# Linear attention and expert-routed gated attention on one core: VectorE splits the low-rank part ahead of the expert state additions, and TensorE computes the next tile's denominators behind the intra-chunk products

## The chip, the cores and the metric

The kernel runs on one core of a Trainium2 chip. The metric is device time in microseconds (us) from launch to end. A core has five engines that run their own instruction streams and meet only at semaphores: TensorE (PE in the rows, PEld for its weight loads), VectorE (DVE), ScalarE (ACT), GpSimd (POOL) and SyncE (SP, which here only issues loads and stores). Within one engine the instructions start in the order in which they are written, so an instruction that waits holds back all that stand behind it.

## The reference, cut to what matters

The input is x of shape 2 x 4096 x 512. Two residual blocks follow each other; `ln` is a layer norm without weights.

```python
x = x + ln(attention(ln(x)))     # linear attention, 16 heads of 32
x = x + ln(ffn(ln(x)))           # gated linear attention with 4 experts

# attention: q, k rectified
z   = 1 / (sum_n(k) . q + eps)                 # the "denominators"
out = (context @ q) * z @ w_proj.T + b_proj

# ffn
q1, k1, v = x @ Wq, x @ Wk, x @ Wv
q2 = x @ Wqa @ Wqb                              # low-rank
k2 = softmax(x @ Wka @ Wkb)
gk1, gk2 = log_sigmoid(x @ Wg1a @ Wg1b + bg1) / 16, log_sigmoid(x @ Wg2a @ Wg2b + bg2) / 16
e = softmax(x @ We); mask = one_hot(top_1(e))   # the router
o = gla(q1, k1, v, gk1) + sum over experts of gla(q2*e*mask, k2*e*mask, v, gk2*mask)
g = x @ Wga @ Wgb
return (rmsnorm(o) * silu(g)) @ Wo
```

`gla` is a recurrence over time, `S_t = diag(exp(gk_t)) S_(t-1) + k_t^T v_t`, `o_t = q_t S_t`. The dense path has one state, and the expert path has four.

## The kernel before, in words

For each of the two batch elements the kernel makes two passes over 32 tiles of 128 rows. The first pass builds keys, moments and queries of the linear attention. The second pass takes one tile after the other and carries the state of the recurrence from tile to tile; it is the pass that the change touches. Its loop body `step(n, p, front, back, ahead)` is written once for each engine and works on three tiles at a time:

- **ahead**, tile n+1: the linear attention's output and the first residual. TensorE computes the denominators (`den`, line 312, into PSUM bank 3), ScalarE turns them into reciprocals (`ahead_z`, lines 647 and 649, as exp(-ln)), VectorE multiplies the queries by them (`ahead_qz`, line 1211), TensorE projects (`y_mm`).
- **front**, tile n: the projections of the second block. TensorE computes the low-rank part (`low_rank`), ScalarE takes it out of PSUM (lines 654 to 656), VectorE splits it into a high and a low fp16 half (`front_low`, lines 1115 to 1122) and routes (`front_router`, lines 1126 to 1145). TensorE's gates (`gates`, line 350) wait for `low_ok`, which VectorE sets at line 1122. `label_bc` (line 346) spreads the router's label over the partitions, VectorE makes masks from it (`front_masks`, line 1151 on), and `project_k` on TensorE waits for these, since it overwrites the label's bank.
- **back**, tile n-1: what the recurrence adds. TensorE multiplies by the states (`inter`, line 448) and by the masked scores (`intra`, line 457), ScalarE squares the result (`back_square`, line 719), VectorE sums, normalises, gates and splits it (lines 1222, 1226, 1230, 1063, 1065), and TensorE transposes it (`og_transpose`, line 466) and projects it (`out_mm`). At the head of a step VectorE masks the scores (`back_masks`, line 1082, `back_masks2`, line 1090) and adds the state products of the dense path (`back_carry1`, line 1099) and of the experts (`back_carry`, line 1106, two instructions of 64 x 1024). GpSimd masks the queries (`back_qm`, line 959) and adds the two score tensors (`back_am`, line 965).

The order of the work is written out by hand: each engine runs its pieces in the order of the calls in its own `step`. On ScalarE that order is `front_ke`, `ahead_z(n + 1)`, `back_square(m)`, `front_sig_high`, `back_rms`. On VectorE it is, behind the router and the masks: `front_kmax`, `front_kdiff`, `front_logsig`, `ahead_qz`, `back_norm`, `front_lslow`, `back_normed`, `back_gated`, `back_split`. The first tile of each batch element runs without back, the last without ahead; 60 of the 64 steps have all three parts, 62 have front and back.

Two semaphore values are set so that a first wait passes: `cur(n)` is n+2 and `prev(n)` is n+1. In `step`, m is n-1 and mp is 1-p.

Of the kernel before, what the change touches and what calls it, by code (L numbers as in the profile page):

```python
# [64 lines left out]
def sandwich_kernel(nc, x_d, wqkv_d, wproj_d, bproj_d, wb_d, wl_d, ws_d, wo_d, nw_d, consts_d, out_d):  # L65
# [11 lines left out]
    with ExitStack() as ctx:  # L77
# [146 lines left out]
        def cur(n):  # L224
            return n + 2
# [69 lines left out]
        def _(pe):  # L295
# [179 lines left out]
            def step(n, p, front=True, back=True, ahead=True):  # L475

                m, mp = n - 1, 1 - p
                if front:
                    low_rank(n)
                    project_v(n)  # L480
                    gates(n)
                    project_k2(n)
                if ahead:
                    den(n + 1, mp)
                if front:
                    label_bc(n)
                if back:
                    inter(m)
                    intra(m, mp)
                if front:  # L490
                    project_k(n)
                    project_q(n)
                if back:
                    og_transpose(m)
                if front:
                    cumulate(n)
                if back:
                    out_mm(m)
                if front:
                    half_sums(n)  # L500
                if ahead:
                    y_mm(n + 1)
                if front:
                    transposes(n)
                    state_products(n, p, ahead)
                    scores(n, 0)
                if ahead:
                    xn_transpose(n + 1)
                if front:
                    scores(n, 1)  # L510
# [521 lines left out]
        def _(dve):  # L1032
# [91 lines left out]
            def front_router(n):  # L1124
                dve.wait_ge(S("low0_ok"), cur(n))
                ve.reduce_max(lmax[:, :], logit_s, X).then_inc(S("lmax_ok"), 1)
                dve.wait_ge(S("lmax_ok"), n + 1)
                ve.tensor_scalar(ldiff[:, :], logit_s, lmax[:, :], None, ALU.subtract).then_inc(S("ldiff_ok"), 1)
                dve.wait_ge(S("ldiff_ok"), n + 1)

                ve.scalar_tensor_tensor(lscore[:, :], ldiff[:, :], 0.0, score, ALU.is_equal, ALU.mult).then_inc(S("lscore_ok"), 1)
                dve.wait_ge(S("lscore_ok"), n + 1)
                ve.reduce_max(lab[:, :], lscore[:, :], X).then_inc(S("lab_ok"), 1)
                dve.wait_ge(S("lab_ok"), n + 1)
                dve.wait_ge(S("rx_pe"), prev(n))
                ve.tensor_scalar(lab_i[:, :], ident, lab[:, :], None, ALU.mult).then_inc(S("labi_ok"), 1)
                dve.wait_ge(S("vm_ok"), prev(n))
                ve.tensor_scalar(m4[:, :], score, lab[:, :], None, ALU.is_equal).then_inc(S("m4_ok"), 1)
                dve.wait_ge(S("m4_ok"), n + 1)
                dve.wait_ge(S("sum_pe"), prev(n))  # L1140
                ve.tensor_tensor(hm[:, :, :], wide(m4[:, :], 2), halves.unsqueeze(1).to_broadcast([P, NEXP, 2]), ALU.mult).then_inc(S("hm_ok"), 1)  # L1141
                dve.wait_ge(S("lexp_ok"), cur(n))
                ve.reciprocal(rr[:, :], lsum[:, :]).then_inc(S("rr_ok"), 1)
                dve.wait_ge(S("rr_ok"), n + 1)
                ve.tensor_scalar(rq[:, :], rr[:, :], D2 ** -0.5, None, ALU.mult).then_inc(S("rq_ok"), 1)
# [97 lines left out]
            def step(n, p, front=True, back=True, ahead=True):  # L1243
                m, mp = n - 1, 1 - p
                if back:
                    back_masks(m)
                    back_carry1(m)
                    back_masks2(m)
                    back_carry(m)
                if front:  # L1250
                    front_low(n)
                    front_router(n)
                    front_masks(n)
                    front_kmax(n)
                    front_kdiff(n)
                    front_logsig(n)
                if ahead:
                    ahead_qz(n + 1, mp)
                if back:
                    back_norm(m)  # L1260
                if front:
                    front_lslow(n)
                if back:
                    back_normed(m, mp)
                    back_gated(m, mp)
                    back_split(m)
                if front:
                    front_kfac(n)
                    front_sil(n, p)
                if ahead:  # L1270
                    ahead_qz_split(n + 1)
                if front:
                    front_gated_1(n)
                    front_gated_q2(n)
                if back:
                    back_out(m, mp)
                if front:
                    front_decay(n, p)
                if ahead:
                    ahead_residual(n + 1, mp)  # L1280
                    ahead_low(n + 1, mp)
# [147 lines left out]
```

## Time and profile before

| | |
|---|---|
| median of 3 runs | 3148.73 us |
| the runs | 3140.97, 3148.92, 3148.73 us |
| the profiled execution | 3142.66 us |
| its span, first to last instruction | 3140.8 us |
| its mean granted TensorE clock | 0.944 of full speed |
| TensorE busy | 2876.9 us (92% of the span) |
| VectorE, ScalarE, GpSimd busy | 1962.6, 1639.7, 1355.5 us |

Some 1.9 us of the profiled execution lie outside its span. Busy times of TensorE are of modelled ends and count work at half clock as busy, so the share of 92% doesn't say that it runs at its peak. The idle time of an engine is listed with what ended it. Where a row names a line, it is the line of the kernel before; after the change the lines of TensorE stand one lower from `inter` on, and those of VectorE one lower up to the router's `hm` and one higher behind it.

### The profile page before, as it was taken

Reading aid. Unit: us, or ns where it says so; the run is one execution under the profiler, and the core shown is the slowest. Engines: PE = TensorE matmul, PEld = TensorE weight load, DVE = VectorE, ACT = ScalarE, POOL = GpSimd, SP = SyncE. Lnnn points to the kernel's source line nnn. Section 1 sums busy time; section 2 is a strip of 40 time slices with the busy share of each in tenths; the row PEclk is TensorE's granted clock in tenths of the full one; section 3 lists DMA queues with packets and bytes.
Section 4 is the critical chain, followed back from the end, with each engine's and each line's share of the span. In section 5 each row is a group of like instructions: output and inputs, shape, how many; then the busy total and the mean of one; then the engine's idle time right before and its main releaser. Section 6 shows DMA issues by size and latency. Waiting matters only on the chain.

```text
span 3140.8 us, 56322 instructions
## 1 busy us (share of the span) xinstructions
PE 2876.9 (92%) x20720; PEld 1830.1 (58%) x20720; DVE 1962.6 (62%) x3878; ACT 1639.7 (52%) x3281; POOL 1355.5 (43%) x1006
## 2 busy tenths in 40 slices
PE   6999899999999999999879988999999999999997
PEld 3444566666666666666534445666666666666665
DVE  4442666667666676666544426666667666666675
ACT  4332555555555565555433325555556555555553
POOL 2873444444444444444322334444444444444443
PEclk9999999999999999999889999999999999999999
DMA  4121000000000000000021110000000000000000
GB/s 171 61 94 41 18 20 20 20 20 20 20 20 20 20 20 20 20 20 20 18 85 57 67 41 18 20 20 20 20 20 20 20 20 20 20 20 20 20 20 11
DMA packets 48376, 97.49 MB, mean 31 GB/s; under 512 B 5376, under 2 KB 5376, under 8 KB 47680
## 3 DMA queue, kind: packets, MB, share of 16 engines
q1 hardware_dynamic: 37008, 68.44, 6.5%
q10 hardware_dynamic: 9792, 17.83, 1.5%
q0 software_dynamic: 1520, 10.50, 0.8%
q8 instruction: 32, 0.52, 0.1%
q14 instruction: 24, 0.20, 0.0%
HBM read 63.19 MB, written 33.55 MB: 31 GB/s over the span
## 4 chain that ended last, share of the span: by engine, by line
PE 77%; DVE 16%; ACT 3%; issue 3%; POOL 1%; DVEq 0%; DMA 0%; POOLq 0%; SPq 0%; ACTq 0%
PE psum L303 12%; PE psum L448 11%; PE psum L304 11%; PE psum L305 11%; PE psum L547 5%; DVE region L1106 5%; PE psum L437 4%; PE psum L312 4%; PE psum L457 4%; PE psum L413 3%; DVE region L1090 3%; PE psum L353 2%; PE psum L423 2%; ACT ogT L730 2%; PE psum L352 2%
## 5 line engine op out<-in xcount | busy, mean ns | idle before, releaser
L977 POOL TENSOR_TENSOR region<-region,kfac 128x512 f32<-128x512 f32 x64 | 66.8, 1043 | 842.3 <-DVE kfac L1190 842.3
L448 PE MATMUL psum<-region 128*128 128x128 f32 x2560 | 352.2, 305 | 10.8 <-POOL region L959 10.8
L448 PEld LDWEIGHTS psum<-region 128*128 128x128 f32 x2560 | 346.1, 221 | 14.5 <-issue 11.1
L959 POOL TENSOR_TENSOR region<-region,mb 128x512 f32<-128x512 f32 x256 | 322.7, 1292 | 73.3 <-ACT region L620 72.9
L992 POOL TENSOR_TENSOR region<-region,decay 64x1280 f32<-64x1280 f32 x128 | 298.3, 2330 | 117.9 <-DVE decay L1206 112.9
L972 POOL TENSOR_SCALAR region<-region,m 128x512 f32<-128x512 f32 x256 | 172.9, 697 | 285.7 <-DVE hm L1141 210.5
L303 PE MATMUL psum<-wb,region 128*128 128x512 f16 x768 | 292.4, 381 | 3.3 <-DVE mb L1155 3.3
L304 PE MATMUL psum<-wb,region 128*128 128x512 f16 x768 | 292.0, 380 | 0.0
L305 PE MATMUL psum<-wb,region 128*128 128x512 f16 x768 | 291.7, 380 | 0.0
L951 POOL TENSOR_TENSOR region<-region 128x1024 f32<-128x1024 f32 x64 | 146.7, 2292 | 287.4 <-DVE region L1302 229.9
L1302 DVE SCALAR_TENSOR_TENSOR region<-psum,region 128x512 f16<-128x512 f32 x64 | 44.3, 692 | 261.0 <-ACT region L791 261.0
L730 ACT ACTIVATE ogT<-psum 128x1024 f16<-128x1024 f16 x64 | 65.5, 1024 | 241.5 <-PE psum L466 241.5
L671 ACT ACTIVATE region<-psum 128x1536 f32<-128x1536 f32 x64 | 92.9, 1452 | 184.7 <-PE psum L353 184.7
L547 PE MATMUL psum<-region 128*128 128x512 f16 x768 | 176.2, 379 | 0.0
L350 PE MATMUL psum<-ws,region 128*128 128x512 f16 x128 | 40.4, 398 | 141.0 <-DVE region L1122 141.0
L1106 DVE TENSOR_TENSOR region<-psum,region 64x1024 f32<-64x1024 f32 x128 | 155.7, 1217 | 0.9
L1072 DVE SCALAR_TENSOR_TENSOR region<-psum,rstd,region 128x512 f32<-128x512 f32 x64 | 48.0, 751 | 170.0 <-ACT rstd L616 170.0
L965 POOL TENSOR_TENSOR region<-region 128x1024 f32<-128x1024 f32 x64 | 150.4, 2350 | 0.0
L423 PE MATMUL psum<-region 64*128 64x128 f32 x2048 | 148.2, 284 | 0.0
L423 PEld LDWEIGHTS psum<-region 64*128 64x128 f32 x2048 | 124.1, 187 | 31.1 <-issue 24.6
L612 ACT ACTIVATE og<-psum 128x512 f32<-128x512 f32 x128 | 76.4, 597 | 123.5 <-PE psum L305 123.5
L620 ACT ACTIVATE region<-psum 128x512 f32<-128x512 f32 x256 | 137.6, 589 | 0.0
(233 smaller groups left out, 7580.7 us busy)
## 6 DMA issues: line engine op xcount, KB each, us to landing
region<-x_in SPq DMA_DIRECT2D x128, 256.0 KB, 2.7
q_cols<-region ACTq DMA_DIRECT2D x64, 256.0 KB, 2.4
region<-q_cols SPq DMA_DIRECT2D x64, 256.0 KB, 2.9
out_rows<-region SPq DMA_DIRECT2D x60, 256.0 KB, 2.0
region<-wb_in POOLq DMA_DIRECT2D x1, 3072.0 KB, 11.2
region<-wqkv_in SPq DMA_DIRECT2D x4, 512.0 KB, 6.2
region<-wqkv_in POOLq DMA_DIRECT2D x2, 1024.0 KB, 5.6
region<-wproj_in POOLq DMA_DIRECT2D x2, 1024.0 KB, 7.4
```

The lines of the kernel that those rows point to most:

```text
L303: mm(out, lhs(0), rhs(0), start=start, stop=False)
L304: mm(out, lhs(0), rhs(1), start=False, stop=False)
L305: return mm(out, lhs(1), rhs(0), start=False, stop=stop)
L423: last = mm(bank[where[odd]][:, pr * P:(pr + 1) * P], kT[h, pr, :], qT[h, pr, :], start=True, stop=True)
L448: last = mm(bank[7][:, pr * P:(pr + 1) * P], q, state[:, pr, path, :], start=(pr == 0 and path == 0), stop=False, skip_group_check=True)
L547: last = mm(bank[4 + j], xn8[:, p * GT + t, x * C + j * P:x * C + (j + 1) * P], k16[:, y_, :], start=first and begins, stop=final and ends ...
L951: nc.gpsimd.tensor_tensor(kacc, kacc, k16, ALU.add).then_inc(S("kacc_ok"), 1)
L959: last = nc.gpsimd.tensor_tensor(qm[:, e, :, :], q2T, mb[:, e, :].unsqueeze(1).to_broadcast([P, PAIRS, P]), ALU.mult)
L965: nc.gpsimd.tensor_tensor(am1[:, :, :, :], am1[:, :, :, :], am2[:, :, :, :], ALU.add).then_inc(S("am_ok"), 1)
L972: last = nc.gpsimd.tensor_scalar(vm[:, e, :], v[:, p, :], m4[:, e:e + 1], 1.0, ALU.mult, ALU.mult)
L992: nc.gpsimd.tensor_tensor(state[h, :, :, h], carry[h, :, :, :], decay[h, :, :].unsqueeze(3).to_broadcast([D2, PAIRS, PATHS, D2]), ALU.mult ...
L1106: last = ve.tensor_tensor(carry[h, :, 1:PATHS, :], psum[h, 2:4, :].rearrange("p a (r e d) -> p (a r) e d", r=2, e=NEXP), state[h, :, 1:PAT ...
```

## The change

It reorders three things in the second pass and changes no instruction. On TensorE, `den(n + 1, mp)` moves from ahead of `label_bc(n)` to behind `intra(m, mp)`. On VectorE, `back_carry(m)` moves from ahead of `front_low(n)` to behind `front_router(n)`. The last two instructions of the router (the reciprocal of the softmax sum and its scaled copy) become `front_prob(n)` and move from ahead of `front_masks(n)` to behind `front_kdiff(n)`. The streams of ScalarE, GpSimd and SyncE are as before.

```diff
--- before.py
+++ after.py
@@ -480,13 +480,12 @@
                     project_v(n)
                     gates(n)
                     project_k2(n)
-                if ahead:
-                    den(n + 1, mp)
-                if front:
                     label_bc(n)
                 if back:
                     inter(m)
                     intra(m, mp)
+                if ahead:
+                    den(n + 1, mp)
                 if front:
                     project_k(n)
                     project_q(n)
@@ -1139,6 +1138,8 @@
                 dve.wait_ge(S("m4_ok"), n + 1)
                 dve.wait_ge(S("sum_pe"), prev(n))
                 ve.tensor_tensor(hm[:, :, :], wide(m4[:, :], 2), halves.unsqueeze(1).to_broadcast([P, NEXP, 2]), ALU.mult).then_inc(S("hm_ok"), 1)
+
+            def front_prob(n):
                 dve.wait_ge(S("lexp_ok"), cur(n))
                 ve.reciprocal(rr[:, :], lsum[:, :]).then_inc(S("rr_ok"), 1)
                 dve.wait_ge(S("rr_ok"), n + 1)
@@ -1246,13 +1247,16 @@
                     back_masks(m)
                     back_carry1(m)
                     back_masks2(m)
-                    back_carry(m)
                 if front:
                     front_low(n)
                     front_router(n)
+                if back:
+                    back_carry(m)
+                if front:
                     front_masks(n)
                     front_kmax(n)
                     front_kdiff(n)
+                    front_prob(n)
                     front_logsig(n)
                 if ahead:
                     ahead_qz(n + 1, mp)
```

TensorE in the loop's body, before, from the last product of `project_k2` on (`kden` are the denominators' weights, `lab_i` the label, `wb` the big projection's weights; a row with no wait named follows from the one above it):

```order
L352 MATMUL psum<-ws,region 128x512 [waits v_ok]
L353 MATMUL psum<-ws,region 128x512
L308 ISA
L312 MATMUL psum<-region,kden 128x128 [waits carry_ok,qb0_in]
L312 MATMUL psum<-region,kden 128x128 x3
L346 MATMUL psum<-lab_i,ones 128x128 [waits am1_ok,labi_ok]
L448 MATMUL psum<-region 128x128 [waits qm_ok,state_ok,out_ok]
L448 MATMUL psum<-region 128x128 x19
L457 MATMUL psum<-region 128x64 [waits am_ok]
L457 MATMUL psum<-region 128x64 x7
L303 MATMUL psum<-wb,region 128x512 [waits mb_ok]
```

The same place after the change:

```order
L352 MATMUL psum<-ws,region 128x512 [waits v_ok]
L353 MATMUL psum<-ws,region 128x512
L346 MATMUL psum<-lab_i,ones 128x128 [waits am1_ok,labi_ok]
L448 MATMUL psum<-region 128x128 [waits qm_ok,state_ok,out_ok]
L448 MATMUL psum<-region 128x128 x19
L457 MATMUL psum<-region 128x64 [waits am_ok]
L457 MATMUL psum<-region 128x64 x7
L308 ISA
L312 MATMUL psum<-region,kden 128x128 [waits carry_ok,qb0_in]
L312 MATMUL psum<-region,kden 128x128 x3
L303 MATMUL psum<-wb,region 128x512 [waits mb_ok]
```

The denominators (L312) stood ahead of the label, the states and the scores; they now stand behind all three and directly ahead of `project_k`, with the wait for `carry_ok` that they carry.

VectorE at the head of the loop's body, before, from the second half of the second score mask on (`low1_ok` is ScalarE's eviction of the low-rank part):

```order
L1090 TENSOR_TENSOR region<-psum,same_c 128x512
L1106 TENSOR_TENSOR region<-psum,region 64x4x256 x2
L1111 REGISTER_ALU
L1115 CAST region<-region 64x2x128 [waits q1_pe,low1_ok]
L1116 CAST region<-region 64x2x128
L1117 CAST region<-region 32x128
```

The same place after the change:

```order
L1089 TENSOR_TENSOR region<-psum,same_c 128x512
L1110 REGISTER_ALU
L1114 CAST region<-region 64x2x128 [waits q1_pe,low1_ok]
L1115 CAST region<-region 64x2x128
L1116 CAST region<-region 32x128
L1119 TENSOR_TENSOR region<-region 32x128 [waits lowh_ok]
```

The expert state additions (L1106) are gone from between the score masks and the first cast, which waits for ScalarE.

VectorE further on, before, from the router's label columns `m` to the log-sigmoid that `project_q` and `front_sig_high` wait for:

```order
L1138 TENSOR_SCALAR m<-cst,lab 128x4 [waits vm_ok]
L1141 TENSOR_TENSOR hm<-m,cst 128x8 [waits sum_pe,m4_ok]
L1143 RECIPROCAL rr<-lsum 128x1 [waits lexp_ok]
L1145 TENSOR_SCALAR rq<-rr 128x1 [waits rr_ok]
L1151 SCALAR_TENSOR_TENSOR same_d<-psum,lab,cst 128x128 [waits cum_pe,rx_pe]
L1152 SCALAR_TENSOR_TENSOR same_c<-psum,lab,cst 128x128
L1155 TENSOR_SCALAR mb<-psum 128x128 [waits qm_ok]
L1155 TENSOR_SCALAR mb<-psum 128x128 x3
L1176 TENSOR_REDUCE kmax<-psum 128x8 [waits k2_pe]
L1182 TENSOR_TENSOR region<-psum,kmax 128x512 [waits k2g_ok,kr_ok,kmax_ok]
L1162 SCALAR_TENSOR_TENSOR region<-psum,region 128x1536 [waits sil_ok,sum_pe,ln_ok]
```

The same place after the change:

```order
L1140 TENSOR_TENSOR hm<-m,cst 128x8 [waits sum_pe,m4_ok]
L1105 TENSOR_TENSOR region<-psum,region 64x4x256 x2
L1152 SCALAR_TENSOR_TENSOR same_d<-psum,lab,cst 128x128 [waits cum_pe,rx_pe]
L1153 SCALAR_TENSOR_TENSOR same_c<-psum,lab,cst 128x128
L1156 TENSOR_SCALAR mb<-psum 128x128 [waits qm_ok]
L1156 TENSOR_SCALAR mb<-psum 128x128 x3
L1177 TENSOR_REDUCE kmax<-psum 128x8 [waits k2_pe]
L1183 TENSOR_TENSOR region<-psum,kmax 128x512 [waits k2g_ok,kr_ok,kmax_ok]
L1144 RECIPROCAL rr<-lsum 128x1 [waits lexp_ok]
L1146 TENSOR_SCALAR rq<-rr 128x1 [waits rr_ok]
L1163 SCALAR_TENSOR_TENSOR region<-psum,region 128x1536 [waits sil_ok,sum_pe,ln_ok]
```

The state additions (now L1105) stand behind `hm`, the router's last step, and ahead of the masks, and the reciprocal that waits for ScalarE's `lexp_ok` stands ahead of the log-sigmoid instead of ahead of the masks.

## Rows read from the trace of the kernel before

**Rows 1.** What line 350 of TensorE waited for: us in all, number of times.
```profile
  DVE region L1122: 141.0, 62
```
**Rows 2.** TensorE in one tile: start, duration, operation [idle before, released by].
```profile
823.92 0.60 PE L350 MATMUL psum<-ws,region 128*128 128x512 f16 x2 [2.28 <-DVE region L1122]
...
825.69 2.07 PE L312 MATMUL psum<-region,kden 128*128 128x128 f32 x8
...
832.78 1.90 PE L457 MATMUL psum<-region 128*128 128x64 f32 x16
...
834.52 0.38 PE L303 MATMUL psum<-wb,region 128*128 128x512 f16 x1
...
840.34 0.61 PE L466 MATMUL psum<-ident,og 128*128 128x128 f16 x8
```
**Rows 3.** VectorE in the same tile, same columns.
```profile
817.70 1.29 DVE L1090 TENSOR_TENSOR region<-psum,same_c 128x512 f32<-128x512 f32 x2
...
818.90 2.45 DVE L1106 TENSOR_TENSOR region<-psum,region 64x1024 f32<-64x1024 f32 x2
...
821.38 0.90 DVE L1115 CAST region<-region 64x256 f16<-64x256 f32 x1
...
823.57 0.29 DVE L1122 TENSOR_TENSOR region<-region 64x128 f16<-64x128 f32 x1
...
825.20 0.17 DVE L1141 TENSOR_TENSOR hm<-m,cst 128x8 f16<-128x8 f32 x1
...
829.93 0.69 DVE L1182 TENSOR_TENSOR region<-psum,kmax 128x512 f32<-128x512 f32 x1
...
830.54 1.75 DVE L1162 SCALAR_TENSOR_TENSOR region<-psum,region 128x1536 f32<-128x1536 f32 x1
```
**Rows 4.** ScalarE in the same tile: the end of the low-rank eviction.
```profile
819.41 0.27 ACT L655 ACTIVATE region<-psum 128x128 f32<-128x128 f32 x1
```
**Rows 5.** GpSimd in the same tile: the sum of the masked scores.
```profile
819.78 2.35 POOL L965 TENSOR_TENSOR region<-region 128x1024 f32<-128x1024 f32 x1
```
**Rows 6.** All 64 instances of line 1115: shortest, median, longest ns, first start.
```profile
L1115 DVE CAST region<-region x64: 285/893/906, 325.5 to 3083.1; 64x256 f16<-64x256 f32 x64
```
**Rows 7.** First pass: all instances of line 1298, same columns.
```profile
L1298 DVE TENSOR_TENSOR region<-region x64: 691/1767/1775, 15.2 to 1817.8; 128x512 f16<-128x512 f32 x64
```
**Rows 8.** First pass, one tile: GpSimd's line 951 and VectorE's line 1298.
```profile
1701.78 2.36 POOL L951 TENSOR_TENSOR region<-region 128x1024 f32<-128x1024 f32 x1 [5.99 <-DVE region L1302]
...
1702.92 1.76 DVE L1298 TENSOR_TENSOR region<-region 128x512 f16<-128x512 f32 x1 [0.77 <-ACT region L804]
```
**Rows 9.** ScalarE in the tile of rows 2: reciprocal denominators and the square.
```profile
831.20 0.64 ACT L647 ACTIVATE psum<-psum,eps_z 128x512 f32<-128x512 f32 x1
...
831.87 0.58 ACT L649 ACTIVATE psum<-psum 128x512 f32<-128x512 f32 x1
...
834.72 0.60 ACT L719 ACTIVATE og<-psum 128x512 f32<-128x512 f32 x1 [2.26 <-PE psum L457]
```
**Rows 10.** VectorE in the same tile: from the denominators to the split output.
```profile
832.49 1.12 DVE L1211 SCALAR_TENSOR_TENSOR region<-region,ksum_q,psum 128x128 f32<-128x128 f32 x4 [0.20 <-ACT psum L649]
...
835.35 0.69 DVE L1222 TENSOR_REDUCE oms<-og 128x8 f32<-128x512 f32 x1 [1.74 <-ACT og L719]
...
837.44 0.68 DVE L1226 TENSOR_TENSOR og<-psum,ors 128x512 f32<-128x512 f32 x1
...
839.34 0.69 DVE L1065 TENSOR_TENSOR og<-og 128x512 f16<-128x512 f32 x1
```
**Rows 11.** Stretches cut where TensorE starts line 350 again: length, TensorE busy, granted clock, DMA share, GB/s.
```profile
358.79:395.47 36.68, 34.13 (x279) 1.00 0.07 23
823.92:862.19 38.27, 35.71 (x278) 0.96 0.06 21
784.12:823.92 39.80, 37.24 (x279) 0.91 0.06 20
358.79:1520.23 1161.44, 1084.88 (x8340) 0.94 0.06 21
```

## The prediction

> **What bounds the kernel now.** I read the page first: TensorE is busy for 92% of the span and leads the chain of waits. I then took the list of what each TensorE line waited for. In the second pass one entry stands out: line 350, the first gate product, waits for line 1122, the last step of VectorE's low-rank split, 62 times for 141.0 us, or 2.27 us a time [rows 1]. The timeline of one tile on the four engines shows how it comes about. TensorE is through with its projection at 821.64 (823.92 less 2.28) and stands until 823.92 [rows 2]. VectorE masks the scores until 818.99, adds the expert states from 818.90 for 2.45 us, and starts the first cast of the split at 821.38; the split ends at 823.86 [rows 3]. The cast's own input is ready earlier: ScalarE ends the eviction at 819.68 [rows 4].
>
> The last view is the granted clock, in stretches cut where line 350 starts again. A tile without any stretch at the lower level (1.2 GHz) takes 36.68 us; others take 38.27 us at a mean of 0.96 and 39.80 us at 0.91 [rows 11]. The clock falls around the time at which TensorE starts again behind the 2.28 us. The mean over the 30 intervals of a batch element is 1161.44 / 30 = 38.71 us, so the halved clock costs 2.0 us a tile over and above the idle time.
>
> So the idle time ahead of the gates costs up to 2.3 us directly and 2.0 us by the clock. Everything behind it hangs on TensorE until the transpose of line 466 at 840.34 [rows 2]. There a second chain arrives nearly at the same time: VectorE's split of the output ends at 839.34 + 0.69 = 840.03 [rows 10]. It has 0.3 us to spare.
>
> **Part 1: VectorE's state additions behind the router.** Their 2.45 us leave the place ahead of the cast. The cast can't start before 819.68, so at best the split starts at 819.7 instead of 821.38.
>
> That supposes that the cast takes its own time only, and this is where I expect the gain to be lost. Of the 64 instances of line 1115 the shortest, the first tile's at 325.5, takes 285 ns, and the median takes 893 ns [rows 6]. In the shown tile it runs from 821.38 to 822.28, and GpSimd's addition of the two score tensors runs from 819.78 to 822.13 [rows 5]; in the first tile there is no such addition. The cast's end is GpSimd's end plus 0.15, which is its own 0.29 less 0.14. The first pass has the same pattern: line 1298 takes 691 ns alone and 1767 ns in the median [rows 7], and in one tile it ends at 1704.68, where GpSimd's line 951 ends at 1704.14 [rows 8]; 1704.14 + 0.69 - 0.14 is 1704.69. I read this as: a VectorE cast, or an addition with both inputs in SBUF, waits until a GpSimd instruction in flight is done.
>
> All six instructions of the split are of these kinds. After the change they are ready at 819.7, where GpSimd starts its 2.35 us. If GpSimd is first, the cast waits until about 821.99 and ends at 822.28, as before. If the cast slips in just ahead (0.29 us), GpSimd, ready since 819.0, takes its turn behind it, and the second cast waits instead, which ends within 0.1 us of where it ended before. Either way `low_ok` comes at 823.86 and the gates start at 823.92. Gain: 0 to 0.1 us; I take 0. If nothing waits, the split takes 2.48 (823.86 - 821.38) less the 0.61 that the cast loses now, and ends at 819.7 + 1.87 = 821.6. The gates then start when TensorE is ready, 2.2 us earlier. That is the other bound: 0 to 2.2 us a tile, besides the clock.
>
> The Trainium skill (SBUF — State Buffer, on the shared port pair) states that VectorE in a two-port mode, or with two SBUF inputs against a GpSimd instruction that reads SBUF, and GpSimd hold a shared port pair exclusively for a whole instruction, and that whoever is second fully blocks. The rows agree with it, to 0.01 us in the first pass. By this rule part 1 gains nothing; by the plain durations it would gain 2.2 us a tile and the clock.
>
> What moves with the additions: they now run from 825.4 (line 1141 ends at 825.37 [rows 3]) to 827.8. They read PSUM and one SBUF tensor, and ran beside GpSimd's addition at 1.22 us each before, so GpSimd's next work does not slow them. Behind them the masks start at about 827.85 instead of 827.9, since VectorE stood there for ScalarE's `lexp_ok` and for the label. The reciprocal pair adds some 0.35 us ahead of the log-sigmoid, where a wait of its own has long been over: that starts at about 830.8 instead of 830.54 [rows 3] and ends at 832.5. Who waits for it is `project_q` at 837 and `front_sig_high`, which is held longer by part 2. Cost: 0.
>
> **Part 2: the denominators behind the scores.** On TensorE nothing is added: the label, the states and the scores start about 1.86 us earlier, the denominators stand last, and `project_k` starts at 834.52 as before [rows 2]. Their end moves from 827.76 to about 834.52 + 0.2 = 834.7, 0.2 being the overlap that the old end had with the next product. The wait for `carry_ok` (827.8) is over by then.
>
> On ScalarE `ahead_z` waits for them, and `back_square` is queued behind it. Before, both halves of `ahead_z` were through by 832.45, and the square started at 834.72, 0.04 us behind the scores [rows 9]. Now it needs, from the denominators' end D: 0.04 for the semaphore, 0.67 to the second activation (831.87 - 831.20), 0.58 for that [rows 9]; the square then follows. VectorE's `ahead_qz` starts at D + 1.33 and holds VectorE for 1.12 us [rows 10], to D + 2.45, behind the square's end (D + 1.9). From there the chain is as before: line 1222 for 0.69, line 1171 for 1.15, and from the start of line 1226 to the end of line 1065 it is 840.03 - 837.44 = 2.59 [rows 10]. The sum is D + 6.88, or some 6.75 with the overlaps of 0.1 between neighbours that do not wait for one another. So `og_ok` comes at 841.45 to 841.6, and TensorE, which is ready for the transpose at 840.34, waits: 1.1 to 1.3 us a tile; I take 1.2. Queued behind that transpose is all the rest of TensorE's tile, and ScalarE and VectorE of that part follow it, so the whole tile is later by this much. The later work has room: the product `y_mm` starts 4.8 us behind the transpose and its input comes 3.3 us behind `og_ok`.
>
> **The sum.** Steps with all three parts: 60. Part 1: 0. Part 2: 60 x 1.2 = +72 us. The first tile of each batch element wins about 1 us, because its label no longer stands behind the denominators: -2. Made against the profiled execution, 3142.66 + 70 = 3213 us. That execution is 6 us below the median of 3148.73; the runs shown spread over 8 us. I forecast 3212.
>
> **What stays open** is the clock. The gap ahead of the gates stays, and so do the halved stretches; but which tile gets none, a short or a long one depends on where its gap falls, and the tile gets 1.2 us longer. If all tiles were of the 36.68 kind the period would be 37.9, which is -0.8 x 60 = -50 us against before; if all were of the 39.80 kind, 41.0 and +137 us. Neither end is likely, and half of each is: the forecast's own range is 3160 to 3265.
>
> **Rivals.**
> - The split is free of GpSimd (faster). The gates start 2.2 us earlier, the gap closes, and the clock stays up. Part 2 still costs its 1.2, since it hangs on the denominators and not on the gates. The tile takes 36.68 - 2.2 + 1.2 = 35.7, that is 3.0 less than 38.71: 3142.66 - 60 x 3.0 = 2963 us. For it: VectorE's six short instructions could keep their turn against a GpSimd instruction not yet begun. Against: rows 6 to 8, and that in the first pass each side gets in between two instructions of the other.
> - The longer wait ahead of the transpose halves the clock once more (slower still). It would join with the 0.25 us behind it. Price: 1.6 us (38.27 - 36.68) a tile for 60 tiles, +95 on the forecast: 3308. It decides when this gap acts like the one of 2.28. Against: no halving follows the 0.25 us.
> - Nothing moves: some 0.3 us of slack and a somewhat shorter gap cancel the new wait, 3143. For it speaks only that VectorE has idle time in each tile.
>
> **How the numbers follow.** Forecast with its own range: 0.74. Free split, or a part of it that spares the clock: 0.15. Clock halved again: 0.05. Nothing moves: 0.06. Less than about 0.3% (9 us) can't be told from no change here. A lucky mix of tiles gives 0.02 of the forecast's share to the faster side. So faster 0.17, same 0.07, slower 0.76. The range leaves out the free split and the second halving and reaches below the forecast's own range towards no change: 3135 to 3265.
>
> **What would show it.** Right: line 1114 still ends with GpSimd's addition, lasting about 2.5 us; line 350 still waits 2.3 us a tile for VectorE; ScalarE's first activation of `ahead_z` waits for TensorE's denominators; and line 465 waits 1.1 to 1.3 us for VectorE's line 1064. Wrong: line 1114 at 0.29 us with its first start at 819.7, a wait ahead of line 350 below 1 us, a granted clock near 1.0, or no wait ahead of line 465.

## The result, and the profile after

The changed kernel takes 3092.02 us in the median of 4 runs (3091.44 to 3092.17), the kernel before 3147.64 us over its 4 (3140.97 to 3148.92). The ratio is 0.9827, with a 95% interval of 0.981 to 0.9844: 55 us or 1.7% faster. The forecast was 3212 us, slower by 2%. It lies on the wrong side, and the measured time lies below the range.

The mean granted clock of the profiled execution, in its line with the span, is the first thing that differs; before it was 0.944:

```profile
core 0: 3090.3 us, clock 0.979
```

What the two lines of TensorE waited for (released by, us in all, times), from the lists of line 350 and of line 466 of the changed kernel. The first answers to [rows 1]:

```profile
  DVE region L1121: 126.1, 62
...
  DVE og L1064: 66.1, 62
```

The same list of line 466 in the kernel before:

```profile
  DVE og L1065: 9.2, 2
```

So the wait ahead of the gates shrank from 2.27 to 2.03 us a tile, no more. The two waits of line 466 that stood before, in the last tile of each batch element, are still there, and a new wait of (66.1 - 9.2) / 60 = 0.95 us stands ahead of the output's transpose in each of the other tiles. The transpose itself starts 1.08 us later: 15.91 us behind line 350 in a tile with the clock up, against 14.83 before. That is the forecast's own picture. TensorE in one tile (start, duration, operation [idle before, released by]), to be read against [rows 2]:

```profile
809.49 0.60 PE L350 MATMUL psum<-ws,region 128*128 128x512 f16 x2 [2.05 <-DVE region L1121]
...
811.26 4.68 PE L448 MATMUL psum<-region 128*128 128x128 f32 x40
...
815.78 1.90 PE L457 MATMUL psum<-region 128*128 128x64 f32 x16
...
817.52 1.11 PE L312 MATMUL psum<-region,kden 128*128 128x128 f32 x8
...
825.39 0.62 PE L466 MATMUL psum<-ident,og 128*128 128x128 f16 x8 [0.95 <-DVE og L1064]
```

The denominators now stand last of the four and take 1.11 us where they took 2.07; in this tile the clock is up. VectorE at the head of the next tile, against [rows 3, 6]:

```profile
841.03 1.29 DVE L1089 TENSOR_TENSOR region<-psum,same_c 128x512 f32<-128x512 f32 x2
...
842.97 0.32 DVE L1114 CAST region<-region 64x256 f16<-64x256 f32 x1 [0.65 <-ACT region L654]
...
843.30 2.35 DVE L1115 CAST region<-region 64x256 f16<-64x256 f32 x1
...
846.64 0.29 DVE L1121 TENSOR_TENSOR region<-region 64x128 f16<-64x128 f32 x1
...
848.26 0.17 DVE L1140 TENSOR_TENSOR hm<-m,cst 128x8 f16<-128x8 f32 x1
...
848.35 2.45 DVE L1105 TENSOR_TENSOR region<-psum,region 64x1024 f32<-64x1024 f32 x2
```

GpSimd's multiplications (line 958) and its addition of the score tensors there, against [rows 5]:

```profile
838.11 5.04 POOL L958 TENSOR_TENSOR region<-region,mb 128x512 f32<-128x512 f32 x4 [1.17 <-ACT region L619]
843.10 2.39 POOL L964 TENSOR_TENSOR region<-region 128x1024 f32<-128x1024 f32 x1
```

The first cast slips in ahead of it, in 0.32 us, and the second lasts 2.35 us, until 845.65: GpSimd's end, 845.49, plus 0.16. The split ends at 846.93, 0.25 us earlier in relation to GpSimd's addition than before (3.83 us behind the addition's start instead of 4.08). All instances of the two casts (shortest, median, longest ns):

```profile
L1114 DVE CAST region<-region x64: 284/285/345, 326.1 to 3031.1; 64x256 f16<-64x256 f32 x64
...
L1115 DVE CAST region<-region x64: 291/2345/2349, 326.4 to 3031.4; 64x256 f16<-64x256 f32 x64
```

ScalarE from the denominators' end on, in the tile of the TensorE rows, against [rows 9]; the square follows the two activations and no longer the scores:

```profile
818.66 0.66 ACT L646 ACTIVATE psum<-psum,eps_z 128x512 f32<-128x512 f32 x1 [1.94 <-PE psum L312]
...
819.36 0.58 ACT L648 ACTIVATE psum<-psum 128x512 f32<-128x512 f32 x1
...
819.85 0.59 ACT L718 ACTIVATE og<-psum 128x512 f32<-128x512 f32 x1
```

VectorE behind it, against [rows 10]:

```profile
819.97 1.12 DVE L1212 SCALAR_TENSOR_TENSOR region<-region,ksum_q,psum 128x128 f32<-128x128 f32 x4 [1.94 <-ACT psum L648]
...
821.01 0.68 DVE L1223 TENSOR_REDUCE oms<-og 128x8 f32<-128x512 f32 x1
...
821.61 1.22 DVE L1172 SCALAR_TENSOR_TENSOR region<-region 128x1024 f16<-128x1024 f32 x1
...
822.74 0.69 DVE L1227 TENSOR_TENSOR og<-psum,ors 128x512 f32<-128x512 f32 x1
...
824.64 0.69 DVE L1064 TENSOR_TENSOR og<-og 128x512 f16<-128x512 f32 x1
```

From the denominators' end at 818.63 to `og_ok` at 825.33 it is 6.70 us; the prediction had 6.75.

What it did not have is the clock. A halving is here a stretch in which the granted clock stands at its lower level, 1.2 GHz. Stretches cut where line 350 starts again (length, TensorE busy, granted clock, DMA share, GB/s), against [rows 11]:

```profile
359.18:396.69 37.51, 34.26 (x279) 1.00 0.06 22
396.69:434.23 37.54, 34.27 (x279) 1.00 0.06 22
1259.78:1300.38 40.60, 37.35 (x279) 0.92 0.06 19
359.18:1495.72 1136.54, 1038.78 (x8341) 0.99 0.06 21
```

A tile with the clock up takes 37.50 to 37.54 us, 0.84 more than the 36.68 of before. But nearly every tile is now of that kind. Sorted by length, the 30 intervals of the first batch element are:

| kernel | clock up | the shorter kind of halving | the longer kind | mean |
|---|---|---|---|---|
| before | 3 at 36.7 | 15 at 38.2 to 38.3 | 12 at 39.8 | 38.71 |
| after | 26 at 37.5 | 1 at 39.0 | 3 at 40.6 | 37.88 |

The halvings sit where TensorE starts again behind the gap ahead of the gates. In one of the long tiles of the changed kernel (same columns; the gap lies in the first stretch) the clock is low in the 8 us behind the restart alone:

```profile
1297.38:1300.38 3.00, 0.97 (x6) 1.00 0.00 0
1300.38:1308.38 8.00, 8.00 (x35) 0.57 0.00 0
1308.38:1341.02 32.64, 29.37 (x246) 1.00 0.07 24
```

Every fall of the clock within the loop comes from 0.1 us ahead of the restart to 2.0 us behind it in the kernel before, and up to 1.0 us behind it in the changed one. None follows the new wait of 0.95 us ahead of the transpose.

The sum: with the clock up, 60 x (37.52 - 36.68) = +50 us. The halvings cost 38.71 - 36.68 = 2.03 us a tile before and 37.88 - 37.52 = 0.36 now: 60 x -1.67 = -100 us. Together -50, and the spans differ by 3090.3 - 3140.8 = -50.5 us.

The helpers that hold the lines of TensorE shown here stand above the edit on TensorE, so lines 350, 448, 457 and 466 all kept their numbers, and do not stand one lower from `inter` on; the 465 in the prediction is line 466.

The third move, `front_prob`, was not run by itself. The lists of waits show no cost of it in the loop: what TensorE waited for the log-sigmoid (line 1163) is 2.7 us in two waits, one in the first tile of each batch element.

### The profile page after: what moved, and what is told of

Its sections match the earlier page's. It is cut to its first block, busy times and chain, and to the rows that moved or that the text cites. A ratio compares the mean times of both kernels' runs of the same rounds, so it can differ in the third digit from the quotient of the medians.

```text
span 3090.3 us, 56322 instructions
## 1 busy us (share of the span) xinstructions
PE 2785.3 (90%) x20720; PEld 1743.0 (56%) x20720; DVE 2041.1 (66%) x3878; ACT 1646.9 (53%) x3281; POOL 1358.3 (44%) x1006
## 4 chain that ended last, share of the span: by engine, by line
PE 71%; DVE 19%; ACT 7%; issue 2%; POOL 1%; DMA 0%; POOLq 0%; ACTq 0%; DVEq 0%; SPq 0%
PE psum L448 10%; PE psum L303 10%; PE psum L305 9%; PE psum L304 9%; PE psum L546 5%; DVE region L1115 5%; PE psum L423 4%; PE psum L437 4%; PE psum L457 4%; PE psum L413 4%; DVE region L1212 2%; DVE region L1172 2%; ACT ogT L729 2%; PE psum L312 2%; PE psum L430 2%
## 5 line engine op out<-in xcount | busy, mean ns | idle before, releaser
L448 PE MATMUL psum<-region 128*128 128x128 f32 x2560 | 317.3, 286 | 10.8 <-POOL region L958 10.8
L448 PEld LDWEIGHTS psum<-region 128*128 128x128 f32 x2560 | 309.1, 202 | 11.1 <-issue 11.1
L1212 DVE SCALAR_TENSOR_TENSOR region<-region,ksum_q,psum 128x128 f32<-128x128 f32 x256 | 71.9, 343 | 138.1 <-ACT psum L648 137.9
L1105 DVE TENSOR_TENSOR region<-psum,region 64x1024 f32<-64x1024 f32 x128 | 155.9, 1218 | 0.9
L350 PE MATMUL psum<-ws,region 128*128 128x512 f16 x128 | 39.8, 393 | 126.1 <-DVE region L1121 126.1
L1115 DVE CAST region<-region 64x256 f16<-64x256 f32 x64 | 146.0, 2281 | 0.9
```

The costliest lines, as they stand in the source:

```text
L448: last = mm(bank[7][:, pr * P:(pr + 1) * P], q, state[:, pr, path, :], start=(pr == 0 and path == 0), stop=False, skip_group_check=True)
L1105: last = ve.tensor_tensor(carry[h, :, 1:PATHS, :], psum[h, 2:4, :].rearrange("p a (r e d) -> p (a r) e d", r=2, e=NEXP), state[h, :, 1:PAT ...
L1115: ve.tensor_copy(low[down, 1:4:2, :], lowf[down, :, :])
```

## The experiments

Three theories stood for the missing halvings. A: whether a gap is followed by a halved clock depends on when it comes in the clock's own course, and so on the tile's period. B: 2.28 us of idle time halves the clock and 2.03 don't. C: it matters what runs behind the gap, and the denominators directly behind the gates made the clock fall. Each time is a median with the ratio to the kernel before, timed beside it, and its 95% interval.

### Each engine's part alone

TensorE's part alone (VectorE's `step` as before):

```diff
-                if ahead:
-                    den(n + 1, mp)
-                if front:
                     label_bc(n)
                 if back:
                     inter(m)
                     intra(m, mp)
+                if ahead:
+                    den(n + 1, mp)
```

> TensorE's part alone: the denominators behind the scores, VectorE as before. All theories: the gap ahead of the gates stays 2.28 us and a new wait of 1.0 to 1.2 us stands ahead of the output's transpose, so a tile without a halved clock takes 36.68 + 1.1 = 37.8 us. Theory A (whether a gap is followed by a halved clock depends on when it comes, so on the tile's period): 37.8 is another period than the changed kernel's 37.5, halvings are as frequent as before or more, 3180 to 3260 us. Theory B (the gap of 2.28 us halves the clock and the one of 2.03 does not): halvings as before, 3142.7 + 66 = 3210 us. Theory C (the denominators directly behind the gates made the clock fall): hardly any halving, 37.8 us a tile, about 3090 us.

Measured: 3212.54 us, 1.0212 (1.0195 to 1.0229). This is the forecast's time, from the half of the change that it blamed. The gap is 2.27 us and the new wait the same as in the changed kernel; a tile with the clock up takes 37.75 us. 22 of 30 tiles have a halving (5 short, 17 long), mean 39.78 us. C falls: the denominators stand last here too. A and B stand.

VectorE's part alone (the same edit undone on TensorE, VectorE's `step` as after the change):

```diff
+                if ahead:
+                    den(n + 1, mp)
+                if front:
                     label_bc(n)
                 if back:
                     inter(m)
                     intra(m, mp)
-                if ahead:
-                    den(n + 1, mp)
```

> VectorE's part alone: split and router ahead of the state additions, denominators where they were. All: gap ahead of the gates about 2.05 us, no wait ahead of the output's transpose, 36.45 us for a tile without a halved clock. A: the period moves from tile to tile against the clock's rhythm as before, so halvings in most tiles, some 1.7 us a tile: 3100 to 3120 us. B: the short gap spares the clock, 3142.7 - 60 x 2.25 = 3008 us. C: halvings as before, 2.0 us a tile, 3125 us.

Measured: 3283.39 us, 1.0436 (1.0418 to 1.0453), far outside all three. TensorE in one tile shows what none of them had counted:

```profile
809.65 0.60 PE L350 MATMUL psum<-ws,region 128*128 128x512 f16 x2 [2.02 <-DVE region L1122]
...
813.61 2.05 PE L312 MATMUL psum<-region,kden 128*128 128x128 f32 x8 [2.18 <-DVE region L1106]
```

The denominators carry the wait for `carry_ok`. With the state additions behind the router that comes later than their old place, and a second gap of 2.18 us opens 1.8 us behind the first. All 30 tiles then have a long halving (40.8 to 41.0 us). So the two halves of the change belong together: moving the denominators behind `intra` is what makes the later state additions free.

### More work on TensorE, nothing else

The sharpest test of A against B adds work and touches neither the gap nor the order. The first product of `y_mm` is repeated, into the same bank, k times; each takes 0.216 us where nothing but TensorE sets the pace.

```diff
                 pe.wait_ge(S("qz_ok"), cur(n))
+                for _ in range(k):
+                    mm(bank[3], ones16[0:HALF, :], bias16[0:HALF, :], start=True, stop=True)
                 mm(bank[3], ones16[0:HALF, :], bias16[0:HALF, :], start=True, stop=False)
```

On the kernel before, k = 4:

> The kernel before with four products repeated ahead of y_mm, 4 x 0.216 = 0.86 us more work on TensorE in every tile, where nothing else limits it; the gap of 2.28 us and the place of the denominators are as before. A: the period without halving becomes 36.68 + 0.86 = 37.54, that of the changed kernel, the halvings go in most tiles, and the kernel gets faster by more work: about 3085 us. B and C: nothing of the clock changes, 3142.7 + 60 x 0.86 = 3194 us.

Measured: 3131.72 us over 6 runs (3101.54 to 3132.57), 0.9953 (0.9937 to 0.997). The kernel is faster with 52 us more of useless work in it. The runs fall into two groups, 3101.5 to 3103.3 and 3131.3 to 3132.6; both are below the kernel before, and neither reaches my 3085. In the profiled execution two tiles in a row read:

```profile
711.56:749.11 37.55, 34.99 (x282) 1.00 0.06 21
749.11:786.65 37.54, 34.99 (x283) 1.00 0.06 21
```

The period is that of the changed kernel, the gap is still 2.27 us and the denominators still stand behind the gates. 26 of 30 tiles have no halving. B and C are refuted by this execution. It took 3103.31 us and belongs to the faster group, which has 2 of the 6 runs; the slower group was not profiled, and its mean clock of 0.967, against 0.977 here and 0.940 to 0.944 in the runs of the kernel before, says only that it too has fewer halvings than before.

On the changed kernel, k = 1:

> The changed kernel with one product repeated ahead of y_mm, 0.22 us more work in every tile; gap of 2.03 us and order unchanged. A: the period becomes 37.74, the halvings come back in most tiles, up to 2.5 us a tile: 3170 to 3250 us, for 13 us of work. B and C: 3092 + 13 = 3105 us, hardly any halving.

Measured: 3198.38 us over 4 runs (3190.4 to 3202.75), 1.0157 (1.0134 to 1.0179). 13 us of work cost 106. Two tiles of it:

```profile
715.71:756.56 40.85, 37.58 (x280) 0.92 0.05 19
874.36:912.12 37.76, 34.48 (x280) 1.00 0.06 21
```

21 of 30 tiles have a halving, with the same gap of 2.04 us.

On the changed kernel, k = 3:

> The changed kernel with three products repeated ahead of y_mm, 0.65 us more work a tile, against 0.22 us in the run with one (3198 us). If every bit of work only adds time: 3198 + 26 = 3224 us. Theory A: the period of a tile without a halved clock becomes 37.52 + 0.65 = 38.17 us, which moves the gap by another step from tile to tile, and stepping the tiles on by the phases read from the earlier runs gives a halving in about every fifth tile, 0.6 us in the mean: some 38.8 us a tile, 3145 to 3165 us, faster than with one product.

Measured: 3156.29 us, 1.0045 (1.003 to 1.0059): 42 us faster than with one product, as A had it. 20 tiles take 38.15 to 38.2 us and 10 take about 39.8: a halving in every third tile, where I had put every fifth.

### The gap filled

If idle time is what lets the clock fall, work of no use in the gap should keep it up. The products follow the gates' own waits for the bank and the last of them, for `low_ok`, follows the products:

```diff
+                pe.wait_ge(S("am1_ok"), prev(n))
+                pe.wait_ge(S("am2_ok"), prev(n))
+                for _ in range(k):
+                    mm(bank[4], xnT[:, 0, 0, :], wb[:, 0, 0, 0:C], start=True, stop=True)
                 pe.wait_ge(S("low_ok"), cur(n))
```

The kernel before, k = 9:

> The kernel before with nine products into a bank that is free there, between the v projection and the gates: 9 x 0.216 = 1.94 us of work of no use inside the gap of 2.28 us. All waits and the order stay. If the idle gap is what halves the clock, no halving is left and every tile takes 36.7 us: 3142.7 - 60 x 2.03 = 3021 us. If the halvings had another cause: 3143 us.

Measured: 3025.70 us, 0.9604 (0.9588 to 0.962). What is left of the gap, from the list of waits (engine, line, released by, us in all, times, longest):

```profile
PE psum L350 <- DVE region L1126: 20.4, 62, 0.3
```

The loop has no halving, and each of its tiles takes 36.7 us.

The changed kernel, k = 8:

> The changed kernel with eight products in the gap ahead of the gates, 1.72 of its 2.03 us; all waits stay. The 8 halvings that the changed kernel still has in the second pass go: 8 x 2.8 = 22 us less, about 3070 us, with a tile of 37.52 us throughout. With the kernel before filled in the same way at 3026 us, this prices the change without the clock: about +45 us, slower by 60 times the difference of 0.95 and 0.23 us.

Measured: 3076.56 us, 0.9788 (0.9771 to 0.9805). With the clock up in both, the changed kernel is slower than the kernel before by 3076.56 - 3025.70 = 51 us, taken across two chips (the kernel before took 3149.45 us on the one and 3143.52 on the other): the forecast's mechanism, less the part that the shorter gap gives back. The loop has no halving here either.

### GpSimd's turn

To test that the split is held by GpSimd's addition, the addition is moved and not the split:

```diff
                 if back:
                     back_qm(n - 1)
-                    back_am(n - 1)
                 if front:
                     front_vm(n, p)
+                if back:
+                    back_am(n - 1)
+                if front:
                     front_k2(n)
```

> The changed kernel with GpSimd's addition of the score tensors behind its expert values instead of ahead of them, so that it no longer runs during VectorE's split; nothing else moves. If a VectorE cast is held by a GpSimd instruction in flight, the split runs free: its second cast takes 0.29 instead of 2.35 us, the gap ahead of the gates falls from 2.03 to below 0.3 us, a tile takes 37.5 - 2.0 = 35.5 us, and with the gap the halvings go: 3092 - 60 x 2.3 = 2950 us. Rival (the second cast is slow by itself or waits for something else): it stays at 2.35 us, the time at 3092 or a little later. Third possibility: the addition now comes too late for the score products, which shows as a wait of line 457 for GpSimd and eats part of the gain.

Measured: 2974.76 us, 0.9443 (0.9427 to 0.9459). All instances of the second cast (line 1117 here; shortest, median, longest ns):

```profile
L1117 DVE CAST region<-region x64: 290/291/292, 325.4 to 2914.7; 64x256 f16<-64x256 f32 x64
```

TensorE in one tile, the gates and the score products, which now wait a little for GpSimd:

```profile
823.61 0.60 PE L350 MATMUL psum<-ws,region 128*128 128x512 f16 x2
...
830.29 2.00 PE L457 MATMUL psum<-region 128*128 128x64 f32 x16 [0.22 <-POOL region L964]
```

Every instance of the cast takes 0.29 us, against a median of 2.35 in the changed kernel, and line 350 no longer waits. The hold is shown, and so is its worth: with the gap gone the loop has no halving but at its ends, though the wait of 0.95 us ahead of the transpose is still there, and the tile takes 36.0 us. That is 0.5 more than the 35.5 that I had put; the third possibility of the expectation accounts for 0.22 of it, and the rest was not traced.

### The square's turn

On ScalarE `back_square` goes ahead of `ahead_z`, on VectorE `back_norm` ahead of `ahead_qz`:

```diff
-                if ahead:
-                    ahead_z(n + 1)
                 if back:
                     back_square(m)
+                if ahead:
+                    ahead_z(n + 1)
```
```diff
-                if ahead:
-                    ahead_qz(n + 1, mp)
                 if back:
                     back_norm(m)
+                if ahead:
+                    ahead_qz(n + 1, mp)
```

> The changed kernel with ScalarE's square ahead of the two activations of the denominators, and VectorE's sum of squares ahead of its product with the denominators. If the new wait of 0.95 us ahead of the output's transpose comes from the square queued behind the denominators, it goes, and a tile without a halved clock takes 37.52 - 0.95 = 36.6 us. Theory A then expects the halvings back in most tiles, since the period has left 37.5: some 38.3 us a tile in the mean, 3115 to 3135 us, slower than the changed kernel although a wait is gone. If halvings were independent of the period: 3092 - 57 = 3035 us.

Measured: 3173.45 us, 1.0073 (1.0056 to 1.009). The wait ahead of the transpose shrank from 0.95 to 0.35 us of idle time, so its cause is the queue behind the denominators, on ScalarE and, for what is left, on VectorE. The kernel is slower than the changed one by 81 us although it waits less: one tile of 30 takes 36.93 us, 14 take 38.4 and 15 take 40.1. The direction is A's; I had stepped the tiles from 36.6 and not from 36.9, and the time is 38 us above the upper end of the expected range.

### Towards a better version

Both edits together:

> Both edits together on the changed kernel: GpSimd's addition late, the square first. No gap that halves the clock is left, so the period no longer matters: 37.5 - 2.0 - 0.95 = 34.6 us a tile, 2895 to 2930 us. If the late addition or the chain that carries the state from tile to tile becomes the limit, the tile stays at 35 us or more: 2940 us and above.

Measured: 2940.19 us, 0.9334 (0.9318 to 0.9349). The tile takes 35.4 us; the 0.35 ahead of the transpose and the 0.23 ahead of line 457 are left.

The last version keeps GpSimd's addition late and moves the denominators' work behind the whole output chain: on ScalarE `ahead_z` behind `front_sig`, on VectorE `ahead_qz` directly ahead of `ahead_qz_split`.

```diff
-                if ahead:
-                    ahead_z(n + 1)
                 if back:
                     back_square(m)
                 if front:
                     front_sig_high(n)
                 if back:
                     back_rms(m)
                 if front:
                     front_sig(n)
+                if ahead:
+                    ahead_z(n + 1)
```
```diff
-                if ahead:
-                    ahead_qz(n + 1, mp)
                 if back:
                     back_norm(m)
 ...
                 if ahead:
+                    ahead_qz(n + 1, mp)
                     ahead_qz_split(n + 1)
```

> The changed kernel with GpSimd's addition late, and on ScalarE and VectorE the denominators' work behind the whole output chain: ScalarE squares, evicts, takes the root and only then inverts the denominators; VectorE multiplies by them just ahead of their split. The wait of 0.35 us that is left ahead of the output's transpose in the kernel with both edits goes: 2940 - 60 x 0.35 = 2919 us. If the denominators then come late for y_mm, a wait ahead of y_mm shows and eats the gain: 2940 us or more.

Measured: 2910.73 us, 0.9262 (0.9246 to 0.9278): the fastest here, 233 us below the kernel before timed beside it (3143.52). The tile takes 34.85 us. What is left of idle time in TensorE's tile:

```profile
846.10 0.60 PE L350 MATMUL psum<-ws,region 128*128 128x512 f16 x2
...
852.80 2.00 PE L457 MATMUL psum<-region 128*128 128x64 f32 x16 [0.23 <-POOL region L964]
...
863.12 0.39 PE L303 MATMUL psum<-wo,ogT 128*128 128x512 f16 x1 [0.25 <-ACT ogT L729]
```

The gates don't wait, the wait ahead of the transpose is gone from the loop, and no new one stands ahead of `y_mm` but 0.55 us in the first tile of each batch element.

## Why the prediction was wrong

**Part 1, the split: the mechanism right, the gain too small.** It said that the split gains 0 to 0.1 us because GpSimd's addition holds it. It gained 0.24. The case in which the first cast slips in ahead is the one that happens: its median is 285 ns. I had let GpSimd's addition start later by that cast's 0.29 us. It lasts 2.39 us in place of 2.35, so its end is later by 0.04 only, and the cast that passes is won. The prediction had taken line 1114 at 0.29 us as the sign of a free split. That sign came, and the split was held all the same, one cast later. The late addition shows the cause by removing it.

**Part 2, the denominators: right.** The chain was put at 6.75 us and measured 6.70. The transpose was put 1.2 us later and starts 1.08 later; the idle time ahead of it, put at 1.1 to 1.3, is 0.95. The square's turn and the last version show its two queues.

**The sum of these: the right sign, 20 us too large, and without the clock.** 60 x (1.08 - 0.24) = +50 us, where the prediction had +70; the tiles with the clock up give +50, and the two filled kernels +51. This error alone would have left the kernel slower.

**What failed is the sentence "The gap ahead of the gates stays, and so do the halved stretches".** The first half of it holds (2.03 us are left of 2.27), the second doesn't. The prediction took 2.0 us of halved clock a tile as a constant that the change leaves alone; it fell to 0.36 us, and that is -100 us. It let the mix of tiles vary by half of its two ends and gave 0.02 to a mix that wins. (Half of the way from 3213 to its ends, 3093 and 3280, is 3153 and 3246, not the 3160 and 3265 put down; the result lies outside either way.) Yet the two ends stood in it: with no halvings, -50 us. The result came out at that end, by a few halvings left and a tile 0.4 us shorter than the 37.9 that I had put: that the number agrees is chance.

The runs show that the length of a tile decides how many gaps are followed by a halving, at the same gap and in the same order. The first batch element of each trace in which this gap is the only one of its size, 30 tiles:

| kernel | gap, us | tile with the clock up, us | tiles with a halving | mean tile, us |
|---|---|---|---|---|
| before | 2.28 | 36.68 | 27 | 38.71 |
| changed, square first | 2.03 | 36.93 | 29 | 39.20 |
| changed | 2.03 | 37.52 | 4 | 37.88 |
| before, 4 products more | 2.28 | 37.54 | 4 | 37.86 |
| changed, 1 product more | 2.03 | 37.74 | 21 | 39.66 |
| TensorE's part alone | 2.27 | 37.75 | 22 | 39.78 |
| changed, 3 products more | 2.03 | 38.17 | 10 | 38.71 |

Two hundredths of a microsecond between two different kernels change nothing, and a quarter of a microsecond decides over nearly two. TensorE's part alone took the forecast's 3212 us because there the assumption happened to hold: 39.78 - 37.75 = 2.03 us of halvings a tile, as before.

My reading of this, which fits the traces but which no run shows by itself: a gap is followed by a halving or not by when it comes in the clock's own course. Before, each tile's length put the next gap elsewhere in it. At 37.52 us the next gap comes almost where the last one came, and that place, once it is a good one, is kept for 20 to 24 tiles; the four long tiles follow in a row, and then it is good again. With 0.22 us more the place moves on each time, and the halvings are back.

The trace that the prediction was made from already showed that this is no matter of chance. Five tiles in a row of the kernel before, cut as in [rows 11]:

```profile
629.51:667.79 38.28, 35.72 (x278) 0.96 0.06 21
667.79:707.57 39.78, 37.23 (x278) 0.91 0.06 20
707.57:745.88 38.31, 35.76 (x278) 0.96 0.06 21
745.88:784.12 38.24, 35.68 (x278) 0.96 0.06 21
784.12:823.92 39.80, 37.24 (x279) 0.91 0.06 20
```

The lengths follow each other in an order that comes again through the whole pass, broken here and there by tiles of 36.68, so a new length had to be expected to give a new order. The terms of the sum were not known to a quarter of a microsecond, so both ends belonged into the range, and faster into the likely outcomes.

**The rivals.** The free split did not come, but priced what is there to win: 2963 was put for it, and the kernel with GpSimd's addition late takes 2975, with a tile of 36.0 us where 35.7 was put. The second halving at the transpose did not come: in the tiles with the clock up it stays up through the wait of 0.95 us. "Nothing moves" did not come either.

What stays open: why a gap at one moment is followed by a halving and at another not. Theory A gave the direction of every run with added work and of the square's turn, but the sizes only in part: the square's turn lies 38 us above its range, the kernel before with four products 17 to 48 us above the 3085 expected, and VectorE's part alone lies outside what any of the three theories gave, because of its second gap. The kernel before with four products falls into two groups of runs 30 us apart; the trace of one run doesn't tell what puts an execution into one or the other.

## What to carry to other kernels

Where each turn of a loop has an idle gap that is sometimes followed by a halved clock, a change's cost per turn is not all of the change's effect: list the lengths of the turns first, and price the change at the turns with the clock up and the halvings apart, as a lottery with two ends. Then close the gap instead of tuning around it: with the gap closed by useful order or even by products of no use, the lottery is gone and times add up again. And when VectorE's first instructions of a critical step are casts, look at what GpSimd runs at that moment before moving them.

## What the runs showed of the hardware that I had not expected

- More work made a kernel faster (52 us of repeated products: -15 us in the median; 3 products instead of 1: -42 us), and 0.22 us a tile more cost 106 us.
- Nine products of no use in an idle gap of 2.28 us took 4.0% off the time (3025.70 against 3149.45 us), because the clock no longer fell.
- A gap of 2.03 us and one of 2.28 us can both be without consequence for the clock or cost another 1.5 to 1.6 or 3.1 us. In the changed kernel the gap costs nothing beyond itself in 26 of 30 tiles.
- A VectorE cast of 64x256 that takes 0.29 us alone lasted 2.35 us behind a GpSimd addition, in the median of 64. The Trainium skill (SBUF — State Buffer, Who interferes with whom) states this exclusive hold; the trace agrees, the held cast ending 0.16 us behind the addition. The trace also shows that VectorE gets in between two instructions of GpSimd, which here lets one cast of three pass: the first starts at 842.97, while the last of GpSimd's multiplications (line 958) runs until 843.15, and is through in 0.32 us.
